# A four-stage transformer kernel: last stage's down product as three split passes, with edits on VectorE's share

## The reference, cut to what matters

```python
scores = jax.nn.sigmoid(x @ Wr)                      # x is x4: T rows of 256
_, idx = lax.top_k(scores + router_bias, TOP_K)      # 2 of 8
w = jnp.take_along_axis(scores, idx, axis=-1)
w = w / (jnp.sum(w, axis=-1, keepdims=True) + 1e-09)
cw = jnp.zeros((T, E)).at[jnp.arange(T)[:, None], idx].add(w)
g = jnp.einsum('th,ehi->tei', x, Wg)                 # 4 experts, 256 -> 128
u = jnp.einsum('th,ehi->tei', x, Wu)
hid = jax.nn.silu(g) * u
mlp_out = jnp.einsum('tei,eih->teh', hid, Wd)        # the down product, 128 -> 256
routed = jnp.einsum('te,teh->th', cw[:, :E_MLP], mlp_out)
# ... plus three shares of x or relu(x), plus a causal convolution of 4 taps
```

## Time and profile before

| what | value |
|---|---|
| time, median of 3 runs | 2256.03 us (2255.97 to 2256.99) |
| span of the profiled execution | 2253.4 us |
| span as the slowest core has it, granted TensorE clock | 2253.4 us, 1.000 |
| TensorE busy | 2227.8 us (99%) |
| VectorE busy | 1771.8 us (79%) |
| ScalarE busy | 1284.9 us (57%) |
| GpSimd busy | 668.4 us (30%) |
| the last stage, per step | 19.5 us |

### The profile page before, as it was taken

The page is one execution under the profiler, slowest core; times in us unless marked ns, Lnnn a source line. Parts: engine busy times, 40 slices in busy tenths (PEclk is TensorE's granted clock), DMA queues, the critical chain, the costliest instruction groups (busy, mean ns, idle before and its releaser), DMA issues. The chain is left out here.

```text
span 2253.4 us, 48207 instructions
## 1 busy us (share of the span) xinstructions
PE 2227.8 (99%) x15396; PEld 1877.8 (83%) x15396; DVE 1771.8 (79%) x6078; ACT 1284.9 (57%) x3250; POOL 668.4 (30%) x1162
## 2 busy tenths in 40 slices
PE   8999999999999999999999999999899999999998
PEld 5777777777777777777799999999788888888887
DVE  5888888888888888888775555555599999999997
ACT  6776777677777777776544333433354554555553
POOL 1123233233233232232220000001355555555542
PEclk9999999999999999999999999999999999999999
DMA  6221010010110010110052222222221121222210
GB/s 235 73 95 31 27 40 30 29 39 29 31 38 27 32 39 27 33 32 27 15 155 85 85 72 80 85 66 69 63 60 60 60 62 54 63 64 64 63 43 19
DMA packets 111641, 129.55 MB, mean 57 GB/s; under 512 B 14898, under 2 KB 98089, under 8 KB 111264
## 3 DMA queue, kind: packets, MB, share of 16 engines
q1 hardware_dynamic: 98249, 105.06, 14.4%
q0 software_dynamic: 12288, 21.21, 3.3%
q10 hardware_dynamic: 855, 0.19, 0.0%
HBM read 84.26 MB, written 54.53 MB: 62 GB/s over the span
## 5 line engine op out<-in xcount | busy, mean ns | idle before, releaser
L715 ACT ACTIVATE a_prob<-a_prob,a_nmax 128x376 f32<-128x376 f32 x512 | 307.0, 604 | 3.4 <-DVE a_nmax L861 3.2
L1440 ACT ACTIVATE e_hidden<-e_first,keep_b 128x256 f32<-128x256 f32 x320 | 134.3, 472 | 282.5 <-PE e_first L80 279.5
L1132 PEld LDWEIGHTS a_turned<-keep_ident,a_prob 128*128 128x128 f32 x1518 | 174.2, 139 | 121.3 <-issue 103.6
L861 DVE CUSTOM_DVE_ANT_0 a_prob<-a_score,a_mask_row 128x376 f32<-128x376 f32 x512 | 262.9, 542 | 13.9 <-DVE r_lg L263 6.2
L1132 PE MATMUL a_turned<-keep_ident,a_prob 128*128 128x128 f32 x1518 | 260.5, 280 | 2.2 <-ACT a_probT L723 1.2
L723 ACT ACTIVATE a_probT<-a_turned 128x384 f32<-128x384 f32 x256 | 125.9, 492 | 221.2 <-PE a_turned L1132 216.1
L80 PE MATMUL e_second<-e_w,e_hidden 128*128 128x256 f32 x1920 | 239.6, 284 | 0.0
L80 PEld LDWEIGHTS e_second<-e_w,e_hidden 128*128 128x128 f32 x1920 | 232.6, 192 | 0.0
L177 POOL TENSOR_SCALAR r_var<-r_mv 128x2 f32<-128x2 f32 x64 | 12.3, 192 | 673.1 <-issue 600.0
L873 DVE TENSOR_SCALAR a_prob<-a_prob,a_rden 128x376 f32<-128x376 f32 x512 | 206.9, 431 | 2.2
L880 DVE COPY a_probT<-a_turned 128x384 f32<-128x384 f32 x250 | 139.2, 557 | 82.6 <-PE a_turned L1132 78.4
(11 more groups left out here) (223 smaller groups left out, 5165.3 us busy)
## 6 DMA issues: line engine op xcount, KB each, us to landing
w_in<-W SPq DMA_DIRECT2D x32, 512.0 KB, 4.0
slots<-a_zeros SPq DMA_DIRECT2D x8, 1280.0 KB, 8.9
keep_rows<-slots SPq DMA_DIRECT2D x40, 256.0 KB, 3.9
answers<-e_y SPq DMA_DIRECT2D x40, 256.0 KB, 2.2
a_xn<-x SPq DMA_DIRECT2D x32, 256.0 KB, 2.9
a_xr<-x SPq DMA_DIRECT2D x32, 256.0 KB, 2.9
x<-r_x SPq DMA_DIRECT2D x32, 256.0 KB, 3.2
w_in<-x SPq DMA_DIRECT2D x32, 256.0 KB, 2.7
```

What stands on the lines that cost most here:

```text
L715: nc.scalar.activation(prob[:, u % 4, a], prob[:, u % 4, a], ACT.Exp, bias=nmax[:, u % 4, a:a + 1], scale=-1.0, accum_out=den[:, u % 4, a: ...
L861: nc.vector.tensor_tensor_reduce(prob[:, u % 4, a], score[SCORE_AT[u][a]][:, 0:NKV], mask_row[:, p], -1.0, 3.0e38, ALU.add, ALU.min, nmax[ ...
L1132: last = nc.tensor.transpose(turned_keys(b, u, a)[0:hi - lo, j], prob[:, u % 4, a, lo:hi], ident[:])
L1440: nc.scalar.activation(hidden[:, 2 * j + i], first[:, j, i * CH:(i + 1) * CH], ACT.Relu, bias=b1[:, 2 * j + i, bass.ds(e, 1)]).then_inc(re ...
```

## The change

Five edits, all in `finish`:

- The down product becomes `split_product` on f32r halves: `wd2` holds both halves of the weights (made once, in step 3: the high half by ScalarE, the low half by VectorE), `hidT` gets a second plane. ScalarE writes the high half as before, and a new VectorE instruction `hidden_low` writes the low one. `down` and the next `gate_up(.., 0)` wait for the low half.
- `normalise4` uses `scalar_tensor_tensor`, with `rs4` broadcast along the row as a second tensor, in place of `tensor_scalar` with two pointer scalars, and stands ahead of `close` in VectorE's step.
- The index cast is gone: `f_oh` compares with the uint32 indices.
- The router's chain has 15 instructions, not 16.
- The second gates, `gate_up(b, 1, 0)`, are written at the start of step s+1 and no longer at the end of step s.

```diff
-        hidT = sb("f_hidT", [P, QT, EM, P])
+        hidT = sb("f_hidT", [P, 2, QT, EM, P], F32R)
+        wd2 = sb("f_wd2", [P, 2, EM, D], F32R)
...
-                nc.scalar.activation(hidT[:, i], gates[i][:].rearrange("p (e s) -> p e s", e=EM), ACT.Copy,
+                nc.scalar.activation(hidT[:, 0, i], gates[i][:].rearrange("p (e s) -> p e s", e=EM), ACT.Copy,
                                      scale=0.5).then_inc(hidT_ok[i], 1)
...
+                if s == 3:
+                    nc.scalar.activation(wd2[:, 0], wd, ACT.Copy).then_inc(wd_high, 1)
...
-                    nc.vector.tensor_scalar(x4h[:, p, i], x3[:, p, i], mv4[:, i, 0:1], rs4[:, i:i + 1],
-                                            ALU.subtract, ALU.mult).then_inc(x4h_ok, 1)
+                    nc.vector.scalar_tensor_tensor(x4h[:, p, i], x3[:, p, i], mv4[:, i, 0:1],
+                                                   rs4[:, i:i + 1].to_broadcast([P, D]),
+                                                   ALU.subtract, ALU.mult).then_inc(x4h_ok, 1)
...
+            def hidden_low(b, i):
+
+                eng.wait_ge(hidT_ok[i], b + 1)
+                nc.vector.scalar_tensor_tensor(hidT[:, 1, i], gates[i][:].rearrange("p (e s) -> p e s", e=EM), 0.5,
+                                               hidT[:, 0, i].bitcast(F32), ALU.mult, ALU.subtract) \
+                    .then_inc(hidT_low[i], 1)
...
-                then(nc.vector.tensor_copy(topf[:], topi[:, :, 0:2]))
-                then(nc.vector.tensor_tensor(oh[:].rearrange("p t k e -> p (t k) e"),
-                                             iota_e[:].unsqueeze(1).to_broadcast([P, QT * 2, E1]),
-                                             topf[:].rearrange("p t k -> p (t k)").unsqueeze(2)
-                                             .to_broadcast([P, QT * 2, E1]), ALU.is_equal))
+                then(nc.vector.tensor_tensor(oh[:],
+                                             iota_e[:].unsqueeze(1).unsqueeze(1).to_broadcast([P, QT, 2, E1]),
+                                             topi[:, :, 0:2].unsqueeze(3).to_broadcast([P, QT, 2, E1]),
+                                             ALU.is_equal))
...
+                if s == 3:
+                    eng.wait_ge(wd_high, 1)
+                    nc.vector.tensor_tensor(wd2[:, 1], wd, wd2[:, 0].bitcast(F32), ALU.subtract).then_inc(wd_low, 1)
                 if live(s - 2):
                     values_out(s - 2)
+                if live(s - 3):
+                    normalise4(s - 3, q)
                 if live(s - 5):
                     close(s - 5, q)
-                if live(s - 3):
-                    normalise4(s - 3, q)
+                if live(s - 4):
+                    hidden_low(s - 4, 0)
...
                     router(s - 3, q)
+                if live(s - 4):
+                    hidden_low(s - 4, 1)
...
-                eng.wait_ge(hidT_ok[i], b + 1)
+                eng.wait_ge(hidT_low[i], b + 1)
...
-                product(total[:, i * D:(i + 1) * D], lambda e: hidT[:, i, e], lambda e: weight("Wd", e), EM,
-                        stop=False).then_inc(down_made[i], 1)
+                split_product(nc, total[:, i * D:(i + 1) * D], lambda a, e: hidT[:, a, i, e],
+                              lambda a, e: wd2[:, a, e], EM, stop=False).then_inc(down_made[i], 1)
...
-                    at_least(eng, hidT_ok[i], b)
+                    at_least(eng, hidT_low[i], b)
...
             def step(s, p):
                 q = 1 - p
+                if live(s - 4):
+                    gate_up(s - 4, 1, 0)
                 if live(s - 2):
                     turn_c(s - 2, p)
...
                 if live(s - 4):
                     add_rest(s - 4, 0)
-                if live(s - 3):
-                    gate_up(s - 3, 1, 0)
```

More of the change, by code:

```diff
@@ L1774, in finish @@
         topi = sb("f_topi", [P, QT, E1], U32)
-        topf = sb("f_topf", [P, QT, 2])
         oh = sb("f_oh", [P, QT, 2, E1])
@@ L1809, in finish @@
             sem("f_" + s) for s in ("own_ok", "x3p_ok", "x4r_ok", "kept_ok", "tap_ok", "cv_ok"))
+        wd_high, wd_low = sem("f_wd_high"), sem("f_wd_low")
+        hidT_low = [sem(f"f_hidT_low{i}") for i in range(QT)]
         gate_made, up_made, th_ok, hs_ok, hid_ok, hid_made, hidT_ok, down_made, total_ok, yo_ok = (
@@ L1815, in finish @@
         yo_out = [sem(f"f_yo_out{i}") for i in range(2)]
-        N_ROUTE = 16
+        N_ROUTE = 15
         N_OWN = 4
@@ L1835, in weight2 @@
             return both[:, :, k]
+        wd = whole[:, LATE_AT["Wd"]:LATE_AT["Wd"] + EM * D].rearrange("p (e d) -> p e d", e=EM)
         def product(out, stationary, moving, tiles, stop=True):
@@ L2268, in down @@
             def down(b, i):
-                eng.wait_ge(hidT_ok[i], b + 1)
+                eng.wait_ge(hidT_low[i], b + 1)
                 if i == 0:
                     at_least(eng, yo_ok, b)
-                product(total[:, i * D:(i + 1) * D], lambda e: hidT[:, i, e], lambda e: weight("Wd", e), EM,
-                        stop=False).then_inc(down_made[i], 1)
+                    if b == 0:
+                        eng.wait_ge(wd_low, 1)
+                split_product(nc, total[:, i * D:(i + 1) * D], lambda a, e: hidT[:, a, i, e],
+                              lambda a, e: wd2[:, a, e], EM, stop=False).then_inc(down_made[i], 1)
             def values(b):
```

## The result

The changed kernel took **2309.8 us** (median of 4 runs, 2308.12 to 2310.63), the kernel before 2256.0 in the same rounds: ratio 1.0237 (95% interval 1.0224 to 1.0249), slower. That is 2.8 us above 2307, the top of the range given for 8 in 10, and at the upper edge of the forecast's own range (2285 to 2310). On two later occasions, told with the experiments, the same kernel took 2298.78 and 2298.64 us.

The account below looks back on a forecast made before the run. TensorE (19.48 us a step) bounded the kernel before, VectorE the changed one: 19.15 + 1.20 + 0.65 - 0.17 = 20.83. 28 steps give +37.2, step 4 +0.8, the end +0.3: 2294 us, 8 in 10 within 2265 to 2307.

Parts of the forecast that it names:

- VectorE sets the step: Full steps: VectorE at 20.83 us alone sets the step, with TensorE at 18.94 having 1.9 us to spare.
- both new kinds are held up by GpSimd: `f_x4h` and `f_oh`, with two SBUF inputs each, wait for GpSimd's large additions: pair 1.81 us, `f_oh` near 0.95.
- VectorE without a wait ahead of `f_cx`: Full steps: the profile would show VectorE not waiting before `f_cx`, with a step period of 20.8 us.
- the `wd2` instructions of step 3: Start of the last stage: the prediction gave these instructions no term.
- the end: Last four steps hide VectorE's additions; one low half (+0.60) stands in the chain against 0.27 saved: +0.3 us.
- the step's sum: VectorE per full step: 19.15 + 1.20 + 0.65 - 0.17 = 20.83 us.
- The low halves: Two `hidden_low` on VectorE per full step, 0.60 us each: +1.20 us, bounds 1.16 and 1.32.
- x4 with `close`: VectorE from `f_x4h` through `close`: 2.47 us in place of 1.82, +0.65, bounds +0.44 and +0.87.
- cast and one-hot: VectorE's router, from cast's old start to `f_cw`: 1.05 us in place of 1.22, -0.17, bounds -0.22 and -0.10.
- all three rivals in which something goes free: New instructions escape GpSimd's hold: both, 2242 us, 11%; only the one-hot, 2271, 7%; only x4, 2266, 5%.
- VectorE's own work: VectorE in a full step of the kernel before: 19.50 less 0.35 us of slack, 19.15 us.
- The second gates written a step later: TensorE's order unchanged, 0 us; gates wait for `hidden_low(1)`, some 0.7 us later, at most 0.1 to 0.2 of a wait.

Follow-up runs that it names:

- The split alone: Kernel before with only the split down product and its place of the gates; old x4, cast and `close` kept: 2287.17 us, ratio 1.0136.
- the moved context product: Changed kernel with TensorE's context product ahead of the first half of the down product: 2297.77 us, on a later occasion 2297.42 us.
- the edit in step 34: Changed kernel with, in step 34 alone, `hidden_low(30, 1)` behind `f_oh` instead of behind the router's last row: 2296.70 us, ratio 1.0181.
- the first move: Changed kernel with GpSimd's `f_x3p` moved behind the shares and `f_x2k` behind the gathers, without waiting for the relu: 2286.18 us, ratio 1.0132.

## Why the prediction was right and wrong

The mechanism was right: VectorE sets the step, and both new kinds are held up by GpSimd. Three steps of the prediction failed: "VectorE without a wait ahead of `f_cx`" (10.4 us on the first occasion, cause open), the `wd2` instructions of step 3, put at nothing (3.0 and 2.5 us), and the end (+6.5 and +8.8 for +0.3). Against them the step's sum was 5.5 us too high, which is luck: it is why the later occasions, 2299, lie so near 2294 although the ends cost 9 to 11 us more than forecast.

**What the new instructions cost.** Right to 0.1 us, and shown one by one. The low halves hold 0.60 each (predicted 0.60); x4 with `close` 2.47 (2.47); cast and one-hot 1.01, from 2122.49 to 2123.50 (1.05), so -0.21 for -0.17. The pair `f_x4h` has one instruction of 0.50 and one of 1.50 us. Its second input is a broadcast of one value a partition, and the one-hot has 32 elements: neither is spared, so all three rivals in which something goes free are excluded by the rows. That GpSimd is what holds them up is shown by moving its additions away: 0.98 us became 0.19 and 1.81 became 0.79. The Trainium skill (SBUF — State Buffer, "Who interferes with whom") has this as a rule: a VectorE instruction with two SBUF inputs contends with a GpSimd instruction that reads SBUF. By the numbers just given the trace agrees.

**VectorE's own work.** Predicted 19.15, measured 19.00 (20.20 with two low halves of 0.60). The slack ahead of `f_cx` was read as 0.35 us and as all there was. It was 0.30 (0.55 from the reciprocal before, 0.25 now), and small lags elsewhere went too once VectorE set the step: `f_x4r` held it 0.62 us before (2116.79 to 2117.41) and holds 0.52 now, the two `f_kshift` 0.35 and now 0.28, the router's last row 0.12 and now 0.08. Together these make up the 0.5 us between 19.49 and 19.00. The sum is 19.00 + 1.20 + 0.65 - 0.21 = 20.64, which is the step on both later occasions and in the fast steps of the first. Predicted was 20.83: 0.19 x 29 = 5.5 us too much.

**"VectorE without a wait ahead of f_cx"** is the step that failed, and on the first occasion alone. 22 of the full steps there had a wait of 0.5 us: 608.8 - 598.4 = 10.4 us. Without it the result is about 2299, inside the range. The program alone does not bring the wait (unedited twice more, none), nor does TensorE's pause behind the context product (0.25 and 0.26 us in the two records), nor the way in (first x3 at 1623.46 and step 3 of 18.65 us on the first occasion, 1623.42 and 18.65 on the third). The split alone has it too, in one step. Its cause stays open: the rival that was named, the gathers that GpSimd issues, was not tested. The chip or the occasion may decide it; the first occasion's chip is not on record, so these can't be told apart.

**The start**: `wd2` was put at nothing, without a reason. Its two instructions stand in front of `f_v`, on which TensorE waits. ScalarE, VectorE and TensorE in step 3 of the changed kernel, first occasion:

```profile
1626.04 1.05 ACT L2054 ACTIVATE f_wd<-late 128x1024 fp32r<-128x1024 f32 x1
1627.12 1.23 DVE L2244 TENSOR_TENSOR f_wd<-late,f_wd 128x1024 fp32r<-128x1024 f32 x1
1628.26 0.42 DVE L2108 TENSOR_TENSOR f_v<-f_bank_c,o_bv 120x256 f32<-120x256 f32 x1
1628.82 1.12 PE L1844 MATMUL f_bank_c<-f_cT,late 128*128 128x120 f32 x8 [1.98 <-DVE f_v L2108]
1631.27 3.12 PE L1844 MATMUL f_bank_x<-f_xT,late 128*128 128x256 f32 x8
```

TensorE stands still 1.98 us there, and the next product of 8 takes 3.12 us where it had 1.89 before. The windows of the second occasion, unedited and then with `wd2` in step 2 (busy us of each engine, then the granted clock), show the reason:

```profile
1622.00:1632.00 10.00, 7.10 (x32) 5.63 (x32) 7.66 (x18) 4.06 (x10) 6.60 (x9) 0.83 0.17 53
```

```profile
1622.00:1632.00 10.00, 7.46 (x41) 5.84 (x42) 7.34 (x21) 4.82 (x13) 6.52 (x9) 1.00 0.21 66
```

The mean granted clock is 0.83 in the one and 1.00, 2.4 GHz throughout, in the other. Of the second occasion's 2.5 us, 1.3 are the later `f_v` (1626.37 - 1621.57 = 4.80 behind the first x3, against 3.50) and 1.2 the slower products behind it (1.12 for 0.66 and 2.65 for 1.89); the edit gives 2.3 back. The first share comes each time, the second does not. The kernel with the moved context product, on the same chip, has the same wait and keeps its clock:

```profile
1627.42 1.12 PE L1844 MATMUL f_bank_c<-f_cT,late 128*128 128x120 f32 x8 [1.98 <-DVE f_v L2108]
1629.44 1.89 PE L1844 MATMUL f_bank_x<-f_xT,late 128*128 128x256 f32 x8
```

Its step 3 is 16.98 us, 1.32 over the kernel before. Of the 13 records with `wd2` in step 3, all with this wait, seven show the lower clock behind it and six do not. All three of the unedited kernel do, neither of the two with the moved context does; what decides it was not taken apart.

**The end**: "the last four steps wait on TensorE and ScalarE and hide VectorE's additions" was wrong, +0.3 for +6.5. The waits of these steps are where VectorE's router is the chain: the second gates stand behind router and low half. TensorE's timeline of the end, first occasion:

```profile
2287.35 1.61 PE L80 MATMUL f_gates<-late,f_x4T 128*128 128x512 f32 x6 [2.07 <-DVE f_hidT L2148]
...
2299.89 2.93 PE L80 MATMUL f_total<-f_wd,f_hidT 128*128 128x256 f32 x12 [0.96 <-DVE f_hidT L2148]
2302.62 0.69 PE L2307 MATMUL f_total<-keep_ident,f_cv 128*128 128x128 f32 x4
```

and in the kernel before:

```profile
2236.30 1.62 PE L80 MATMUL f_gates<-late,f_x4T 128*128 128x512 f32 x6 [0.33 <-ACT f_hidT L1981]
```

From the 31st x3 to these gates it is 36.4 us, against 33.0 (2236.30 - 2203.30): +3.4. To the last down product it is +5.5, and this product itself takes 2.73 us (2299.89 to 2302.62) where the one before took 1.83: +0.9. That the low half behind the router delays these gates is shown by the edit in step 34, 0.94 us of the 3.4; how the rest divides between the low halves on the chain and the clock was not taken apart. The second occasion's +8.8 has the down product behind the gates at the lower clock too (2.73 us for 1.59).

**The second gates written a step later**: 0 us by TensorE's order, right. The wait of 1 to 2 us that was forecast for TensorE ahead of them is there, 25.3 us in 21 steps on the second occasion and 34.5 on the first, and VectorE, which sets the step, does not wait for it in the full steps. That it is on the path at the end is the part that was missed.

## What to carry to other kernels

Here an instruction that a big GpSimd addition held up was not helped by another kind with two SBUF inputs, however short: look at what runs on GpSimd at that instant and move that, then look at what it meets in its new place, since here the first move put the hold on the relu. Price an edit at the ends of a pipeline separately: there a wait that the full steps hide stands on the path and can take TensorE's clock with it, and one-time preparations belong where the engines wait anyway. And before a stall is put down to the program, run the unedited program again beside the cure: here the cure "won" 12 us only against another occasion. Nor does a gain of 2 us in one execution prove an edit at the end, where one kernel's own executions lay 2 us apart.

## What the runs showed of the hardware

- One TENSOR_TENSOR of 128x32 took 0.98 us beside a GpSimd addition of 128x512 and 0.19 alone; `f_x4h`, whose second operand is a broadcast of one value a partition, was held up all the same (1.50 us for 0.47).
- The same wait of TensorE, 1.98 us in step 3, was followed by a lower granted clock in seven records (0.83 over 10 us on the second occasion, a product of 1.89 us taking 2.65) and by none in the other six. At the end, after a wait of 2.08 us, the unedited kernel's next product took 1.59 and 1.60 us on two occasions and 2.73 on a third; after 1.14 us it took 1.60 in both records. The length of the wait alone does not say what the clock does.
- The same program had a wait of 0.5 us on a TensorE result in 22 of 28 steps on one occasion and in none on two others, with the other engines' starts around it equal within 0.02 us: 10 us, 0.45% of the time, that no edit explains.
